# Edge placing spread over recall's steps, GpSimd's fills taken out of the second attention's norm, and another order of transposes and loads

## The reference

```python
h = _L0_tok_ref(...)                       # token mixing
h = h + _L0_attn_ref(_layernorm(h), ...)   # windowed attention
h = h + _L0_ffn_ref(_layernorm(h), ...)    # product-key memory, then causal attention over its results
h = h + _L1_attn_ref(_layernorm(h), ...)   # full attention, 8 heads of 8 channels
h = h + _L1_ffn_ref(_layernorm(h), ...)    # graph attention over 262144 edges as a gate, 4 experts

def _L1_attn_ref(x, Wq, bq, Wk, bk, Wv, bv, Wo, bo):
    q, k, v = x @ Wq.T + bq, x @ Wk.T + bk, x @ Wv.T + bv      # then split into 8 heads
    attn = softmax(einsum('bhnd,bhmd->bhnm', q, k) * SCALE)
    return einsum('bhnm,bhmd->bhnd', attn, v)... @ Wo.T + bo
```

## Time and profile before

| | |
|---|---|
| median of 3 executions | 5409.38 us (5408.78 to 5412.29) |
| profiled execution, device time | 5418.73 us |
| span of its trace | 5417.1 us |
| busy in the span | PE 83%, DVE 65%, ACT 40%, POOL 18% |
| recall | from 2974 us of the span |
| place() | 3837.8 to 3847.0 us |
| heads, norm and first maxima | 3850.7 to 3946.4 us |
| heads, loop over 36 tiles | 3946.4 to 4857 us |

### The profile page before, as it was taken

The page is one execution under the profiler, slowest core; times in us unless marked ns, Lnnn a source line. Parts: engine busy times, 40 slices in busy tenths (PEclk is TensorE's granted clock), DMA queues, the critical chain, the costliest instruction groups (busy, mean ns, idle before and its releaser), DMA issues. The chain is left out here.

```text
span 5417.1 us, 70716 instructions
## 1 busy us (share of the span) xinstructions
PE 4511.5 (83%) x24566; PEld 2741.0 (51%) x24566; DVE 3539.8 (65%) x8754; ACT 2168.9 (40%) x3709; POOL 964.3 (18%) x1111
## 2 busy tenths in 40 slices
PE   7797899999999999999999799989599999961004
PEld 3463344444444444444454455555388989861002
DVE  7546677777777776777655577776655555774325
ACT  1352344444444444444444454455234344320001
POOL 0123111111111111111000000000233320005771
PEclk8555899999999999999999799999599999985556
DMA  2004454656454545564643411010110010000110
GB/s 70 8 1 100 99 138 120 134 117 144 119 148 119 142 120 127 118 126 127 149 116 100 134 36 36 24 36 1 30 20 16 6 20 7 6 2 7 20 14 12
DMA packets 324608, 389.23 MB, mean 72 GB/s; under 512 B 119821, under 2 KB 274713, under 8 KB 323456
## 3 DMA queue, kind: packets, MB, share of 16 engines
q1 hardware_dynamic: 233956, 186.63, 17.2%
q0 software_dynamic: 58224, 171.28, 10.4%
q10 hardware_dynamic: 32076, 26.80, 2.7%
HBM read 313.90 MB, written 70.64 MB: 71 GB/s over the span
## 5 line engine op out<-in xcount | busy, mean ns | idle before, releaser
L1072 PE MATMUL mem_kv<-mem_weights,mem_table 128*128 128x456 f32 x4608 | 1957.1, 546 | 0.0
L1340 DVE SCALAR_TENSOR_TENSOR mem_weights<-mem_above,mem_exps 128x912 f32<-128x912 f32 x1152 | 1273.8, 1106 | 690.8 <-ACT mem_exps L1217 687.8
L1217 ACT ACTIVATE mem_exps<-mem_above 128x912 f32<-128x912 f32 x1152 | 1071.2, 931 | 935.1 <-PE mem_above L1059 934.5
L1072 PEld LDWEIGHTS mem_kv<-mem_weights,mem_table 128*128 128x128 f32 x4608 | 871.7, 189 | 567.7 <-issue 452.0
L1059 PE MATMUL mem_above<-mem_operands,mem_selector 123*128 123x456 bf16 x2304 | 637.1, 357 | 60.7 <-DMA mem_inv_z<-scratch_inv_z 35.4
L2270 DVE TENSOR_REDUCE mha_chunk_max<-mha_max_scores 114x1 f32<-114x342 f32 x864 | 439.5, 513 | 309.8 <-PE mha_max_scores L2042 290.1
L2065 PE MATMUL mha_sums<-mha_probs,mha_value_wide 114*72 114x114 f32 (+1 forms) x5184 | 607.9, 261 | 14.2 <-ACT mha_probs L2252 14.2
L2065 PEld LDWEIGHTS mha_sums<-mha_probs,mha_value_wide 114*72 114x72 f32 (+1 forms) x5184 | 559.9, 143 | 23.2 <-issue 21.0
L1059 PEld LDWEIGHTS mem_above<-mem_operands,mem_selector 123*128 123x128 bf16 x2304 | 218.4, 98 | 579.0 <-issue 465.1
L2252 ACT ACTIVATE mha_probs<-mha_scores 114x912 f32<-114x912 f32 x324 | 298.1, 931 | 383.3 <-PE mha_scores L2054 374.3
L960 POOL DMA_DIRECT2D mem_table<-in_L_ffn_tables_dram x288 | 154.0, 540 | 1368.9 <-PE mem_kv L1072 1363.6
(11 more groups left out here) (593 smaller groups left out, 5294.7 us busy)
## 6 DMA issues: line engine op xcount, KB each, us to landing
mem_table<-in_L_ffn_tables_dram POOLq DMA_DIRECT2D x288, 512.0 KB
mem_operands<-scratch_second_scores SPq DMA_DIRECT2D x216, 256.5 KB
mem_operands<-scratch_first_scores SPq DMA_DIRECT2D x288, 128.2 KB
mem_inv_z<-scratch_inv_z SPq DMA_DIRECT2D x72, 228.0 KB
scratch_second_scores<-mem_sel_parts ACTq DMA_DIRECT2D x81, 171.0 KB
scratch_first_scores<-mem_sel_parts ACTq DMA_DIRECT2D x108, 114.0 KB
scratch_mem_q<-mem_weights SPq DMA_DIRECT2D x16, 513.0 KB, 6.0
scratch_mem_keys<-mem_kvT SPq DMA_DIRECT2D x72, 114.0 KB, 9.5
```

The lines of the kernel that those rows point to most:

```text
L1072: last = nc.tensor.matmul(acc[k][:, 0:SPAN], table[:, k, ch, :], W[:, J % 3, c, :], start=(ch == 0), stop=(ch == CHUNKS - 1))
L1217: nc.scalar.activation(E[:, J % 2, :, :], psD[J % 2][:, :, 0:SPAN], ACT.Exp).then_inc(exped, 1)
L1340: nc.vector.scalar_tensor_tensor(W[:, J % 3, :, :], psD[J % 2][:, :, 0:SPAN], 0.0, E[:, J % 2, :, :], ALU.is_ge, ALU.mult).then_inc(weight ...
```

## The change

- `place()` becomes a generator that gives way after each linked instruction. From round 14 on (`PLACE_FROM = 2 * 21 // 3`), VectorE takes one of them at the end of each step; the 28 are through by step 9 of round 15, and nothing of it is left behind the steps.
- GpSimd's fills leave the norm. It only builds `sel` there and writes the small index tables. The three `qs` buffers and `mparts` are zeroed by VectorE behind `centre(1)`. Rows 64 to 127 of both `keys` buffers come by transfers: ScalarE copies `sel` out to `seed` (64 x 2736, bf16), and SyncE moves `seed` into `keys` with six transfers of 64 x 8 x 342. `Vw[0]` is zeroed after the last `split_qk`.
- The first keys are loaded from GpSimd's queue and no longer from SyncE's.
- TensorE turns image `b + 1` before it projects image `b`; ScalarE's copies follow.
- SyncE's queue has one `load(u)` between two `store_parts(b)` instead of nine loads behind the first.

```diff
+        PLACE_FROM = 2 * FIRST_ROUNDS // len(SEARCH_AT)
...
-            dve.wait_ge(estep, FIRST_ROUNDS * EXTRACT_STEPS)
-            place()
+                    if p >= PLACE_FROM:
+                        next(placing, None)
...
 @block.gpsimd
+            nc.gpsimd.memset(sel[:, :], 0.0).then_inc(sel_done, 1)
+            for i in range(PARTS):
+                pool.wait_ge(sel_done, i + 1)
+                nc.gpsimd.affine_select(out=sel[:, :], ...).then_inc(sel_done, 1)
...
-            nc.gpsimd.memset(keys[0][64:96, :, :], 0.0).then_inc(pinit, 1)
-            for k in range(QBUFS):
-                nc.gpsimd.memset(qs[k][64:128, :, :], 0.0).then_inc(pinit, 1)
...
-            nc.gpsimd.memset(Vw[0][:, :, :, :], 0.0).then_inc(zeroed, 1)
-            set_selector(0)
-            nc.gpsimd.memset(keys[1][64:96, :, :], 0.0).then_inc(pinit, 1)
-            set_selector(1)
...
+                pool.wait_ge(k_st[b], 16)
+                pool.wait_ge(seeded[b % 2], 16 * 3)
+                for i in range(PARTS):
+                    nc.gpsimd.dma_start(keys[b % 2][i * 24:(i + 1) * 24, :, :], ...).then_inc(k_in[b % 2], 16)
+                if b < 2:
+                    pool.wait_ge(pstep, BATCH * PROJ_STEPS)
...
+                    nc.gpsimd.memset(Vw[b][:, :, :, :], 0.0).then_inc(zeroed, 1)
...
 @block.sync
+            sp.wait_ge(sel_set, 1)
+            for k in range(2):
+                for c in range(3):
+                    sp.dma_start(keys[k][64:128, :, c * HALF:(c + 1) * HALF], seed[64:128, :, :]).then_inc(seeded[k], 16)
...
             store_parts(0)
-            for i in range(PARTS):
-                sp.dma_start(keys[0][i * 24:(i + 1) * 24, :, :], ...).then_inc(k_first, 16)
             sp.wait_ge(q_st[0], 16 * PARTS)
-            for u in range(QBUFS):
-                load(u)
-            for b in range(1, BATCH):
-                store_parts(b)
+            load(0)
+            store_parts(1)
+            load(1)
+            store_parts(2)
+            load(2)
+            store_parts(3)
...
 @block.scalar
+            act.wait_ge(sel_done, PARTS + 1)
+            nc.scalar.activation(seed[64:128, :, :], bc_free(sel[64:128, :], 64, HALF), ACT.Copy).then_inc(sel_set, 1)
             square(0)
...
 @block.vector
             centre(0)
             centre(1)
+            for k in range(QBUFS):
+                nc.vector.memset(qs[k][64:128, :, :], 0.0).then_inc(pinit, 1)
+            nc.vector.memset(mparts[:, :], 0.0).then_inc(pinit, 1)
             spread(0)
```

More of the change, by code:

```diff
@@ L1732, in one_hots, with place @@
                                             ALU.is_equal).then_inc(hot, 1)
+            def place():
+                V = nc.vector
+                st = Steps(dve, splaced)
+                dve.wait_ge(eiota, 5)
+                dve.wait_ge(estep, FIRST_ROUNDS * EXTRACT_STEPS)
+                L = edge.found[:, 0:FIRST]
+                valid, t, r, rem, same, k, ok = (ew[:, n, :] for n in range(7))
+                per = float(UNITS * NODES)
+                st.link(V.tensor_scalar(valid, L, -SHIFT - 1.0, None, ALU.is_gt))
+                yield
+                st.link(V.tensor_scalar(t, L, -SHIFT, None, ALU.max))
+                yield
+                st.link(V.tensor_scalar(r, t, 1.0 / per, SHIFT / per - 0.5, ALU.mult, ALU.add))
+                yield
+                st.link(V.tensor_scalar(r, r, MAGIC, MAGIC, ALU.add, ALU.subtract))
+                yield
+                st.link(V.tensor_scalar(rem, r, per, SHIFT, ALU.mult, ALU.subtract))
+                yield
+                st.link(V.tensor_tensor(rem, t, rem, ALU.subtract))
+                yield
+                st.link(V.tensor_scalar(t, rem, 0.0, None, ALU.is_lt))
+                yield
+                st.link(V.tensor_tensor(r, r, t, ALU.subtract))
+                yield
+                st.link(V.scalar_tensor_tensor(rem, t, per, rem, ALU.mult, ALU.add))
+                yield
+                st.link(V.tensor_scalar(t, rem, per, None, ALU.is_ge))
+                yield
+                st.link(V.tensor_tensor(r, r, t, ALU.add))
+                yield
+                st.mark(V.memset(same[:, 0:1], 0.0))
+                st.link(V.tensor_tensor(same[:, 1:FIRST], r[:, 1:FIRST], r[:, 0:FIRST - 1], ALU.is_equal))
+                yield
+                st.link(V.scalar_tensor_tensor(same, same, -1.0, eoff[:, 1, :], ALU.add, ALU.mult))
+                yield
+                st.link(V.tensor_scalar(same, same, -1.0, None, ALU.mult))
+                yield
+                st.link(V.tensor_tensor_scan(t, same, same, 0.0, ALU.max, ALU.max))
+                yield
+                st.link(V.tensor_tensor(k, eoff[:, 1, :], t, ALU.subtract))
+                yield
+                st.link(V.tensor_scalar(ok, k, float(CELL), None, ALU.is_lt))
+                yield
+                st.link(V.tensor_tensor(ok, ok, valid, ALU.mult))
+                yield
+                st.link(V.tensor_scalar(k, k, ew[:, 7, 0:1], None, ALU.add))
+                yield
+                st.link(V.scalar_tensor_tensor(k, r, float(128 * CELL), k, ALU.mult, ALU.add))
+                yield
+                st.link(V.tensor_tensor(k, k, eoff[:, 0, :], ALU.subtract))
+                yield
+                st.link(V.tensor_tensor(k, k, ok, ALU.mult))
+                yield
+                st.link(V.tensor_tensor(edge.place[:, :], k, eoff[:, 0, :], ALU.add))
+                yield
+                over = edge.late[:, ECOLS:ECOLS + FIRST]
+                st.link(V.tensor_tensor(t, valid, ok, ALU.subtract))
+                yield
+                st.link(V.tensor_tensor(over, L, t, ALU.mult))
+                yield
+                st.link(V.tensor_scalar(t, t, -SENTINEL, SENTINEL, ALU.mult, ALU.add))
+                yield
+                st.link(V.tensor_tensor(over, over, t, ALU.add))
+                yield
@@ L1734, in _ @@
+            placing = place()
             nc.vector.memset(edge.late[:, ECOLS + FIRST:LATE], SENTINEL).then_inc(init, 1)
@@ L1906, in heads_stage @@
             o.sem(n) for n in ("w_in", "small_set", "scaled", "pool_set", "sel_done", "selector_set"))
[L1907 removed]
+        identb_set = o.sem("identity_set")
+        seeded = [o.sem(f"keys_seeded{k}") for k in range(2)]
         nstep, centred, squared, var_done, root_done, normed, nturned, x_cp = (
@@ L2105, in project_v @@
                                         wv[:, :], start=True, stop=True)
-            for b in range(BATCH):
-                turn_normed(b)
-                if b == 0:
-                    pe.wait_ge(w_in, 16 * 8)
-                    pe.wait_ge(scaled, 1)
-                project_qk(b)
+            turn_normed(0)
+            turn_normed(1)
+            pe.wait_ge(w_in, 16 * 8)
+            pe.wait_ge(scaled, 1)
+            project_qk(0)
+            turn_normed(2)
+            project_qk(1)
+            turn_normed(3)
+            project_qk(2)
+            project_qk(3)
             for t in range(TILES):
@@ L2435 @@
 QBUFS = 3
-PINIT = 3 + QBUFS
 SCATTERS = 3
```

102 lines of the change are left out of this document (22 added, 80 removed).

## The result

The changed kernel takes 5374.07 us (median of 4 runs, 5372.03 to 5385.15) against 5409.08 us (4 runs, 5407.38 to 5412.29): a ratio of 0.9936, 95% interval 0.9922 to 0.9951, 35.0 us less. Its profiled execution took 5372.03 us with a span of 5370.4 us, 46.7 us under the profiled execution of before.

What follows compares the result with a forecast made beforehand. TensorE bounds recall and the loop; between them place(), a norm held up by GpSimd, and stores and loads set the time. 9.2 + 20.9 + 4.7 = 34.8 us off 5409.4 gives 5374.6 us, range 5368 to 5392.

Steps and rivals of the forecast that it cites:

- place(): End of recall: 9.2 us on VectorE behind the steps goes, instructions added in the steps cost 0; gain 0 to 9.2.
- rival 4: Recall's rounds 14 and 15: longer TensorE gaps keep its clock at 0.50, 80 us more, 5455 us; chance 0.02.
- rival 3: Recall's steps: place()'s instructions make TensorE wait, up to the full 9.2 us back, 5384 us; chance 0.07.
- Hold-ups: Norm: VectorE instructions held up by GpSimd's fills and copies get back 23.3 us; 20.9 us net after costs.
- ScalarE's copy to `seed`: Norm: 2.7 us for 2736 columns, ending by 3.9 us, before a square is wanted at 5.0; barely hidden.
- The seeds: SyncE's queue: six transfers, 2.1 MB at 136 GB/s, end at 21.5 us before the first store; cost 0.
- Transfers: Stores and loads before image 3's split: 28.4 us become 23.7 with three loads between, gain 4.7 us (to 9.7).
- I take the two as independent: Stores and loads: the first keys' load on GpSimd's queue was taken not to slow SyncE's q stores.
- Rival 1: Stores and loads: keys' load or seeds delay the stores, 5 to 9 or up to 13 us, 5383 us; chance 0.17.
- Rival 2: Stores and loads: faster landings shorten the chain 5 us, then projections and copies limit; 5369 us; chance 0.10.
- Chain to the first score: From image 3's split to the first score: searches, maxima and turn unchanged at 22.8 us.
- The signs that I named: Changed profile: short TENSOR_SCALARs, first CAST at 19 to 20 us, 24 and 22.8 us stretches, loop same within 3 us.

Runs made afterwards that it cites:

- run 1: Kernel before with place() alone spread over the steps of rounds 14 and 15: 5424.59 us against 5434.17, ratio 0.9984.
- run 2: Kernel before with GpSimd's fills alone moved out of the norm, orders and keys' queue as before: 5412.14 us, ratio 0.9969.
- run 6: Changed kernel with GpSimd's fill of Vw[0] put back into the norm, behind the index tables: 5377.23 us in one run.
- run 9: Kernel before with the norm's eight TENSOR_SCALARs on 114x9 written as SCALAR_TENSOR_TENSOR, GpSimd's fills in place: 5404.8 us in one run.
- run 3: Changed kernel with before's order of transposes and projections in the norm: 5397.15 us, ratio 0.9936.
- the control: Changed kernel unedited, on the chip of some of the other runs: 5366.49 us against 5408.46, ratio 0.9925.
- run 5: Changed kernel with the first keys loaded from SyncE's queue again: 5375.91 us in one run against 5410.45.
- run 4: Changed kernel with before's nine loads of q behind the first store: 5395.86 us, ratio 0.9937.
- run 8: Changed kernel with four buffers of parts instead of two, so no split waits for a store's landing: span 2.8 us shorter, 5369.3 us in one run.
- run 11: Changed kernel with four buffers of parts and image 1's keys loaded behind the zeroing of Vw[1]: 5364.57 us, ratio 0.992.

## Right or wrong, step by step

**place(), booked at 9.2 us.** Right: 9.1 us on the path, and 0.4 us for the instructions in rounds 14 and 15 (run 1). The traces show 27 linked instructions and the small fill, so 27 steps take one and not 28; they last 0.24 to 0.34 us, but for one scan of 0.51. Not foreseen: 1.5 us less at recall's end, through TensorE's clock. It is rival 4's mechanism with the other sign and a small size. Rivals 3 and 4 are out; the changed rounds keep their clock of 0.93.

**Hold-ups, booked at 23.3 us.** The cause was right: runs 2 and 6 show it from both sides, and run 9 shows which form is held by what. The norm's gain is 21.6 us for the 20.9 forecast. The parts of that were off in opposite directions. The free rows were taken at 0.33 and about 1.0 us where they are 0.17 and 0.86 to 0.96, so the hold-ups were worth 24.2 us (20.3 for the three long ones, 3.7 for the two pairs, 0.2 for the rows of 0.33 and 0.20) and not 23.3. VectorE's fills took 1.51 us and not 1.3. That leaves 22.7 us, as its busy time says (40.44 to 17.74). Of this 1.1 us went to more idle time. I had booked 1.1 us for just such a wait, and put it down to TensorE's new order; that was wrong, as the old order loses 1.0 us of it as well (run 3). The right size of this term is luck.

**ScalarE's copy to `seed`, booked as hidden.** It took 2.48 us (2.7 worked out), and VectorE's first reduction of a square starts at 3842.61 us, right behind its fills. Right.

**The seeds, booked at 0 with 2 us of cover.** Landed 19.7 us after the stage's start (21.5 worked out), since they moved at some 152 GB/s and not 136; cover 3.2 us.

**Transfers, booked at 4.7 us.** 4.2 in this trace, 3.8 in the control. The sum hides two errors: the loads between the stores were booked at 2.3 us and took 4.2, and the second landing, booked at 10.8 from issue to split, took 9.1. The first error is the step "I take the two as independent". They aren't: the keys' load from GpSimd's queue costs 1.2 to 1.7 us (run 5), and some 2.6 with the old order of loads (run 4). That the second, 1.7 us the other way, made up for it is luck. Rival 1 was thus a true mechanism at a fifth of its price. Rival 2's better landings came in part, and its next limit, image 3's split not before 39 us, is what run 8 reached, at 37.1.

**Chain to the first score, 22.8 us:** 22.75, the same within 0.3 us in all twelve runs. `Vw[0]`'s fill is hidden there as booked.

**The sum, 34.8 us:** 35.0 between the medians. The traces give 36.0 for the stretches that the change touches. The interval of the ratio stands for 26 to 42 us, so the times alone would not tell this sum from one that is 7 us off; the stretches do.

**The signs that I named.** The TENSOR_SCALARs, the 24 us from the first store to the split that waits, and the 22.8 us behind it came as said. The first CAST came at 18.9 us and not at 19 to 20. The loop was 4.6 us shorter, not the same within 3 us; runs with the same loop differ by up to 7.

## What to carry to other kernels

When a small VectorE instruction takes as long as a GpSimd instruction beside it, add up by how much each is too long, and move GpSimd's work out of the stretch; changing the form of the held one handed most of the wait to the next here (run 9). A buffer that waits for a landing is to be looked at first in such a chain (two more buffers took 10 us off it), but then look at what shares its memory and its queue: the 6.5 us that the loop took back were gone once one load was issued later. And where a chip's runs scatter by 10 us, parts of 1 to 7 us are read from stretches of the trace and not from the total. How well a stretch repeats has to be looked up first: the norm repeated to 0.02 us, the transfers to 0.4 us in one kernel and 1.8 in another.

## What the runs showed of the hardware that I had not expected

- Issuing a transfer can itself take long when much is under way: six seeds took 9.98 us to issue, the last three q stores 10.97 us in run 8 and image 2's three 10.88 us in run 6, both while image 1's keys were loaded from the other queue, and the last three 2.94 us in run 11 with that queue quiet.
- The low clock at the end of recall lasted 20.5 us in the kernel before and in runs 2 and 9, and 17.1 us in all eleven traces with the spread `place()`. A change of VectorE's list alone moved it (run 1).
- GpSimd's 4.96-us fill let a reduction pass at full speed (0.74 us) and held the next instruction, a TENSOR_SCALAR on 9 columns, to its end (run 6). The wait stands in the instruction's own duration, not in the idle time before it.
- The three fills of 64x456 uint32 took 1.40 us together, 0.47 each; the 1024 numbers of the earlier trace rows took 912 ns, so by that row 456 elements would take 0.41 us and 912 of them 0.81: the halved count is what fits. The Trainium skill, "VectorE: DVE Perf Modes", "Zero memsets can be issued as uint32 (trn2)", says so of zeros.
